# Latent attention: another order of TensorE's blocks in a step, and VectorE's front pieces moved

## The chip, the cores and the metric

The kernel runs on one core of one Trainium2 chip. The metric is the device time of one execution in microseconds; lower is better. TensorE (PE) multiplies matrices, its weight loads are shown as PEld; VectorE (DVE), ScalarE (ACT) and GpSimd (POOL) work element by element; SyncE (SP) issues the transfers. The engines run their own instruction queues in order and wait for one another on semaphores.

## The reference, cut to what matters

Two transformer layers run over x (16 sequences of 128 rows, 256 columns). The change touches the attention of the second one, and a part of the feed-forward's front that runs beside it.

```python
# x: (16, 128, 256), kv_c: (16, 128, 64); H = 16 heads, K = 128, D_C = 64, D_CQ = 192, R = 64
q_hk  = (layernorm(x) @ Wq.T)                      # per head 128
q_big = rope(einsum('bshk,hkq->bshq', q_hk, w_kc_q))   # per head 192
q_r   = einsum('bshq,hqr->bhsr', q_big, W_qr)
k_r   = einsum('bld,hdr->bhlr', rope(kv_c), W_kr)
attn  = softmax(einsum('bhsr,bhlr->bhsl', q_r, k_r))
ctx_c = einsum('bhsl,bld->bhsd', attn, rope(kv_c))
x    += einsum('bhsd,hkd->bhsk', ctx_c, w_kc_kv) @ Wo.T
# then: layernorm(x), quantised in blocks of 32 values (the "front"), and a feed-forward
```

## The kernel before

`latent_attention` folds the weights of each head: `a` is Wq times w_kc_q, `b` is W_qr times W_kr (so that keys need no projection of their own), `wc` is w_kc_kv times Wo. A step n handles one pair of heads for one group of four sequences: 8 pairs by 4 groups make 32 steps, and the loop over n has three more for what is still under way.

In a step TensorE computes three tiles of queries (`tile`, six matmuls each over 512 columns, as products of high and low parts). VectorE multiplies them by the rotary tables (`rotate_both` for tiles 0 and 1, `rotate_last`), GpSimd adds the products up (`add`), and in the next step TensorE makes the narrow product with `b` (`narrow_product`, 64 rows of output per head). ScalarE copies it to `qs` (`keep_narrow`, line 1446). Then come the scores (`score`, 64 rows of contraction per head), VectorE's maxima (`maximum`), ScalarE's exponentials (`exponential`), VectorE's reciprocals (`invert`), GpSimd's normalisation; TensorE transposes the probabilities (`turn_p`), ScalarE copies them (`keep_p`), TensorE multiplies them by the context (`context`, 64 rows of output per head), ScalarE copies the result and VectorE subtracts the copy, which leaves the low part (`keep_context`, `split_context`), and TensorE applies `wc` (`project`), accumulating over the eight pairs in two banks.

The order of the work is written out by hand, one list for each engine. Before, TensorE's list is

```python
                tile(n, 0); tile(n, 1); spare(n, 0); tile(n, 2); narrow_product(n - 1); spare(n, 1)
                turn_p(n - 2, 0); project(n - 3, 0); turn_p(n - 2, 1); project(n - 3, 1); spare(n, 2)
                score(n - 1); context(n - 2); spare(n, 3)
```

(the lines are joined here). `spare` holds what only some steps have. In steps 0 to 6 it folds the next pair's weights at its four places, each copied by ScalarE and split by VectorE before the next may use the one bank `w_ps`: queries' weights in two halves (`queries_weights`), context weights (`context_weights`, 64 rows of output per head), narrow weights. In steps 7, 15 and 23 it transposes the next group's rows in two halves (`turn`, `keep_rows`, `split_rows`). In steps 17, 25 and 33 it transposes the front's rows.

The front of group j is made in pieces, at fixed steps k after 8(j+1): VectorE's addition of the output to x (`f.add`, 2), statistics (3), with GpSimd's `deviations` (3), ScalarE's `f.normalise` (5), VectorE's block scales (6), division (7), clip and product (8), TensorE's transposes (9). Before, VectorE's pieces stand at the end of a step. ScalarE also normalises the next group's rows for this attention, in steps 1, 9 and 17 (`normalise`, line 1419). The front of the last group falls into the stage after.

Of the kernel before, what the change touches and what calls it, by code (L numbers as in the profile page):

```python
# [1128 lines left out]
def latent_attention(nc, m, f, d):  # L1129
# [6 lines left out]
    with ExitStack() as scope:  # L1136
# [20 lines left out]
        q_ps, w_ps = m.bank(6), m.bank(7)  # L1157
        ctx_ps, rows_ps = q_ps, m.ps16[:, 1, :]


        tile_bank = lambda n, k: (changing[n % 2], m.bank(1), changing[(n + 1) % 2])[k]
        scores_bank = lambda n, head: (changing[(n + 1) % 2], m.bank(3))[head]
        turned_p_bank = lambda n, head: (changing[n % 2], m.bank(3))[head]
        rows = [slice(0, CE), slice(CE, 2 * CE)]
# [19 lines left out]
        @block.sync  # L1184
        def _(sp):
            load_narrow(sp, m, d, 0)
            for i in range(1, PAIRS):
                wait(sp, c_made, i - 1)
                load_wide(sp, m, d, i)
                wait(sp, b_made, i - 1)  # L1190
                load_narrow(sp, m, d, i)

        @block.tensor
        def _(pe):
# [42 lines left out]
            def spare(n, place):  # L1237

                i, j, fj = weights_in(n), rows_in(n), front_in(n, 9)
                if i is not None:  # L1240
                    if place == 0:
                        wait(pe, b_kept, i)
                        if i == 1:
                            pe.wait_ge(y_lo, 1)
                        queries_weights(i, 0, w_ps)
                    elif place == 1:
                        pe.wait_ge(a_lo, 2 * i + 1)
                        queries_weights(i, 1, w_ps)
                    elif place == 2:
                        pe.wait_ge(a_lo, 2 * i + 2)  # L1250
                        context_weights(i, w_ps)
                    else:
                        pe.wait_ge(c_lo, i + 1)
                        narrow_weights(i, w_ps)
                if j is not None and place < 2:
# [5 lines left out]
                    turn(j, place, w_ps)  # L1261
                if fj is not None and place == 0:
                    pe.wait_ge(y_lo, 2 * min(fj + 2, GROUPS - 1) + 2)
                    f.turn(pe, m, fj, rows_ps)

            def tile(n, k):

                if inside(n, STEPS):
# [4 lines left out]
                    if k == 0 and i == 0:  # L1273
                        pe.wait_ge(y_lo, 2 * j + 2)
                    if k == 2:
                        if n == 0:
                            pe.wait_ge(c_lo, 1)
                        wait(pe, exp_made[0], n - 1)
                    else:
                        wait(pe, tile_turned, t - 2 * k)  # L1280
                    for kin in range(HALVES):
# [6 lines left out]
            def narrow_product(n):  # L1288

                if inside(n, STEPS):  # L1290
# [3 lines left out]
                    pe.wait_ge(q_made, 2 * n + 2)  # L1294
                    wait(pe, cs_lo, n - 1)
                    for head in range(2):
                        pe.matmul(q_ps[rows[head], :], b[i][:, 0, head * CE:(head + 1) * CE], q[n % 2][:, head, :],
                                  start=True, stop=False)
                    pe.matmul(q_ps, b[i][:, 1, :], q[n % 2][:, 2, :], start=False, stop=True).then_inc(narrowed, 1)  # L1299

            def turn_p(n, head):

                if inside(n, STEPS):
                    pe.wait_ge(normed[head], n + 1)
                    if head == 0:
                        pe.wait_ge(tile_turned, min(TILES * (n + 2) + 1, TILES * STEPS))
                    for s in range(4):
# [22 lines left out]
            def score(n):  # L1330

                if inside(n, STEPS):
                    if n == 0:
                        pe.wait_ge(c_lo, 1)
                    pe.wait_ge(qs_made, n + 1)
                    pe.wait_ge(tile_turned, min(TILES * (n + 1) + 1, TILES * STEPS))
                    for s in range(4):
                        for head in range(2):
                            if s == 0:
                                wait(pe, p_kept[head], n)  # L1340
                            t = pe.matmul(scores_bank(n, head)[:, s * S:(s + 1) * S], qs[rows[head], s * S:(s + 1) * S],  # L1341
# [4 lines left out]
            def context(n):  # L1346

                if inside(n, STEPS):
                    wait(pe, cs_lo, n)
                    for s in range(4):  # L1350
                        for head in range(2):
# [12 lines left out]
            for n in RUN:  # L1364
                tile(n, 0)
                tile(n, 1)
                spare(n, 0)
                tile(n, 2)
                narrow_product(n - 1)
                spare(n, 1)  # L1370
                turn_p(n - 2, 0)
                project(n - 3, 0)
                turn_p(n - 2, 1)
                project(n - 3, 1)
                spare(n, 2)
                score(n - 1)
                context(n - 2)
                spare(n, 3)

        @block.scalar  # L1380
        def _(act):
# [17 lines left out]
            def spare(n, place):  # L1399
                i, j, fj = weights_in(n), rows_in(n), front_in(n, 9)  # L1400
                if i is not None:
                    if place < 2:
                        keep_queries_weights(i, place, w_ps)
                    elif place == 2:
# [3 lines left out]
                if j is not None and place < 2:  # L1408
                    keep_rows(j, place, w_ps)
                if fj is not None and place == 0:  # L1410
                    f.keep(act, fj, rows_ps)
# [49 lines left out]
            for n in RUN:  # L1461
                exponential(n - 2, 0)
                keep_context(n - 3)
                exponential(n - 2, 1)
                spare(n, 0)
                keep_narrow(n - 1)
                spare(n, 1)
                keep_p(n - 2, 0)
                keep_p(n - 2, 1)
# [8 lines left out]
        def _(dve):  # L1478
# [21 lines left out]
            def spare(n, place):  # L1500
                i, j = weights_in(n), rows_in(n)
                if i is not None:
                    if place < 2:
                        split_queries_weights(i, place, w_ps)
                    elif place == 2:
                        split_context_weights(i, w_ps)
                if j is not None and place < 2:
                    split_rows(j, place, w_ps)

# [59 lines left out]
            for n in RUN:  # L1569
                maximum(n - 2, 0)  # L1570
                maximum(n - 2, 1)
                rotate_both(n, 0)
                invert(n - 2, 0)
                split_context(n - 3)
                rotate_both(n, 1)
                invert(n - 2, 1)
                spare(n, 0)
                rotate_last(n)
                spare(n, 1)
                spare(n, 2)  # L1580
                if n == 0:
                    last_statistics()
                for k, part in ((2, f.add), (3, f.statistics), (6, f.scales), (7, f.divide), (8, f.clip), (8, f.multiply)):
                    if front_in(n, k) is not None:
                        part(dve, m, front_in(n, k))

        @block.gpsimd
        def _(pool):
# [24 lines left out]
            for n in RUN:  # L1613
# [3 lines left out]
                if n == 0:  # L1617
# [6 lines left out]
                    pool.wait_ge(var_made, 4)  # L1624
                if front_in(n, 3) is not None:
                    f.deviations(pool, m, front_in(n, 3))
                    pool.wait_ge(f.var_made, VAR_STEPS * (front_in(n, 3) + 1))

# [560 lines left out]
```

## Time and profile before

| | |
|---|---|
| median of 3 runs | 831.03 us (829.92 to 831.12) |
| profiled execution | 830.3 us, of which the span from first to last instruction is 828.5 us |
| mean granted TensorE clock | 0.979 |
| latent stage, first tile to the start of the next stage | 352.6 to 741.2 us |

Times in the trace count from the span's first instruction. A matmul's record in the trace shows its form as rows\*columns of the array that its weights take, then the moving data as partitions x columns. Records of matmuls overlap, since they are pipelined, so the distance of one start to the next tells what a matmul costs, not its duration. A matmul in plain fp32 has two records.

### The profile page before, as it was taken

Reading aid. Unit: us, or ns where it says so; the run is one execution under the profiler, and the core shown is the slowest. Engines: PE = TensorE matmul, PEld = TensorE weight load, DVE = VectorE, ACT = ScalarE, POOL = GpSimd, SP = SyncE. Lnnn points to the kernel's source line nnn. Section 1 sums busy time; section 2 is a strip of 40 time slices with the busy share of each in tenths; the row PEclk is TensorE's granted clock in tenths of the full one; section 3 lists DMA queues with packets and bytes.
Section 4 is the critical chain, followed back from the end, with each engine's and each line's share of the span. In section 5 each row is a group of like instructions: output and inputs, shape, how many; then the busy total and the mean of one; then the engine's idle time right before and its main releaser. Section 6 shows DMA issues by size and latency. Waiting matters only on the chain. (4 is left out here: it accounts for less than half of the span.)

```text
span 828.5 us, 14817 instructions
## 1 busy us (share of the span) xinstructions
PE 754.8 (91%) x4808; PEld 539.7 (65%) x4808; DVE 611.7 (74%) x1083; ACT 403.6 (49%) x1068; POOL 571.5 (69%) x590
## 2 busy tenths in 40 slices
PE   4999999869999999788999999999999999876786
PEld 2555555447878887666777777777777777652564
DVE  5898999867887878665656666776678675749994
ACT  1688888533223222216545454655455445454453
POOL 5667776336676757555656778788877887817996
PEclk9999999989999999989999999999999999998999
DMA  9200000040000010122110000000000000000001
GB/s 258 109 1 0 0 0 1 2 169 20 20 19 20 19 57 0 51 103 96 48 49 1 1 1 1 2 2 1 1 1 1 2 1 1 1 2 7 25 32 40
DMA packets 8763, 24.12 MB, mean 29 GB/s; under 512 B 1711, under 2 KB 5167, under 8 KB 8087
## 3 DMA queue, kind: packets, MB, share of 16 engines
q1 hardware_dynamic: 8154, 23.28, 8.5%
q8 instruction: 33, 0.54, 0.3%
q14 instruction: 27, 0.22, 0.1%
q10 hardware_dynamic: 549, 0.08, 0.1%
HBM read 21.26 MB, written 2.10 MB: 28 GB/s over the span
## 5 line engine op out<-in xcount | busy, mean ns | idle before, releaser
L1606 POOL TENSOR_TENSOR q<-turned 64x512 f32<-64x512 f32 x128 | 168.1, 1313 | 25.7 <-DVE turned L1532 9.5
L1283 PE MATMUL ps<-l_yt,a 128*128 128x512 f32 x576 | 145.6, 403 | 2.1 <-ACT p L1429 1.6
L1283 PEld LDWEIGHTS ps<-l_yt,a 128*128 128x128 f32 x576 | 106.2, 190 | 27.4 <-issue 4.7
L1593 POOL TENSOR_TENSOR p<-p,l_inverse 128x512 f32<-128x512 f32 x64 | 66.8, 1047 | 74.2 <-DVE l_inverse L1554 73.7
L1429 ACT ACTIVATE p<-ps,l_negmax 128x128 f32<-128x128 f32 x256 | 91.1, 382 | 43.2 <-DVE l_negmax L1523 43.2
L1532 DVE TENSOR_TENSOR turned<-ps,rope 128x1024 f32<-128x1024 f32 x64 | 78.1, 1220 | 44.5 <-PE ps L1283 41.9
L871 PE MATMUL ps<-yt_experts,wsplit 128*128 (+1 forms) x384 | 99.2, 409 | 5.7 <-DVE h L974 5.2
L467 DVE TENSOR_REDUCE negmax<-ps 128x4 f32<-128x512 f32 x128 | 84.3, 685 | 12.9 <-PE ps L290 12.3
L871 PEld LDWEIGHTS ps<-yt_experts,wsplit 128*128 128x128 f32 x384 | 72.4, 195 | 23.6 <-issue 5.4
L383 ACT ACTIVATE pt<-ps 128x512 f32<-128x512 f32 x128 | 71.0, 599 | 6.3 <-PE ps L312 4.0
L1523 DVE TENSOR_REDUCE l_negmax<-ps 128x4 f32<-128x512 f32 x64 | 41.2, 686 | 44.3 <-PE ps L1341 44.1
L1544 DVE TENSOR_TENSOR turned<-ps,rope 64x512 f32<-64x512 f32 (+1 forms) x96 | 65.5, 683 | 2.1 <-PE ps L1283 0.7
L1446 ACT ACTIVATE qs<-ps 128x512 f32<-128x512 f32 x32 | 19.1, 597 | 98.1 <-PE ps L1299 98.1
L1073 POOL TENSOR_TENSOR ht<-h,ht 128x512 fp32r<-128x512 f32 x32 | 44.7, 1398 | 27.5 <-ACT ht L937 27.1
L1323 PE MATMUL ps<-wc,cs 128*128 128x256 f32 x384 | 62.0, 298 | 1.4 <-DVE cs L1560 1.4
L290 PE MATMUL ps<-bd,qt 96*128 96x512 f32 x128 | 56.5, 483 | 4.2 <-DVE negmax L467 2.6
L937 ACT ACTIVATE ht<-h 128x512 fp32r<-128x512 f32 x32 | 20.2, 632 | 80.2 <-DVE h L974 77.9
L894 PE MATMUL ps<-wsplit,ht 128*128 128x256 f32 x384 | 52.9, 288 | 6.7 <-POOL ht L1073 5.4
L894 PEld LDWEIGHTS ps<-wsplit,ht 128*128 128x128 f32 x384 | 50.7, 195 | 11.6 <-POOL ht L1073 7.6
L1429 ACT ACTIVATION_READ_ACCUMULATOR p<-ps,l_negmax 128x1 f32 x256 | 56.9, 222 | 0.0
L1323 PEld LDWEIGHTS ps<-wc,cs 128*128 128x128 f32 x384 | 50.5, 192 | 1.7 <-DVE cs L1560 1.7
L312 PE MATMUL ps<-qt,bd 104*128 104x512 f32 x128 | 51.6, 429 | 0.0
(213 smaller groups left out, 1567.0 us busy)
## 6 DMA issues: line engine op xcount, KB each, us to landing
wide<-in_wide SPq DMA_DIRECT2D x8, 768.0 KB, 4.5
mx_raw<-in_mx SPq DMA_DIRECT2D x8, 384.0 KB, 3.1
x<-in_x SPq DMA_DIRECT2D x4, 512.0 KB, 8.9
ctx_t<-in_ctx_t SPq DMA_DIRECT2D x1, 2048.0 KB, 7.6
out<-x SPq DMA_DIRECT2D x16, 128.0 KB, 1.7
narrow<-in_narrow SPq DMA_DIRECT2D x8, 192.0 KB, 2.6
ktraw<-in_ctx_rows SPq DMA_DIRECT2D x1, 1248.0 KB
wraw<-in_gate SPq DMA_DIRECT2D x1, 1024.0 KB, 18.4
```

The source lines that it names most:

```text
L290: pe.matmul(scores[k % 2], qt[par][0:QROWS, half, g, :], bd[par][0:QROWS, half, :, :].rearrange("p k t -> p (k t)"), start=True, stop=True ...
L383: act.activation(pt[i][:, :], scores_t[i % 3], ACT.Exp, scale=scale).then_inc(exp_made, 1)
L467: dve.tensor_reduce(negmax[par][:, g, half * KV4:(half + 1) * KV4], scores[k % 2].rearrange("s (k t) -> s k t", k=KV4), AX.X, ALU.max, neg ...
L871: t = pe.matmul(out, w_at(pw, w + k * EXPERTS * INTER + x * INTER, INTER), run_of(m.yt[:, py, k, :, :], j).rearrange("p b s -> p (b s)"), ...
L894: t = pe.matmul(down_ps[:, s, :], ht[par][:, ph, s * S:(s + 1) * S], w_at(pw, 4 * FFN + expert * E, E), start=(expert == 0 and q == 0 and ...
L1283: out = pe.matmul(tile_bank(n, k), a[i][:, pa, kin, k * 128:(k + 1) * 128], yt[j % 2][:, py, kin, :, :].rearrange("p b s -> p (b s)"), sta ...
L1323: t = pe.matmul(proj_ps[:, half, s * E:(s + 1) * E], cs[n % 2][:, pc, (2 * half + s) * S:(2 * half + s + 1) * S], wc[:, pw, i, :], start=( ...
L1429: t = act.activation(p[:, head, s, :], scores_bank(n, head)[:, s * S:(s + 1) * S], ACT.Exp, bias=negmax[:, head, s:s + 1], accum_out=total ...
L1532: dve.tensor_tensor(turned[:, 2 * k:2 * k + 2, :].rearrange("p t (b s) -> p t b s", b=4), spread(tile_bank(n, k).rearrange("p (b s) -> p b ...
L1544: r = dve.tensor_tensor(turned[out_rows, k, :].rearrange("p (b s) -> p b s", b=4), tile_bank(n, 2)[in_rows, :].rearrange("p (b s) -> p b s ...
L1593: pool.tensor_tensor(p[:, head, :, :], p[:, head, :, :], spread(inverse[:, head, :], 2, S), ALU.mult).then_inc(normed[head], 1)
L1606: t = pool.tensor_tensor(out[rows[(head + half) % 2], head, :], turned[rows[head], half, :], turned[rows[head], 2 + half, :], ALU.add)
```

## The change

TensorE's list becomes: tiles 0 and 1, spare 0, tile 2, narrow product of step n-1, spare 1, context of n-3, scores of n-1, both transposes of probabilities of n-2, spare 2, both outputs of n-3, spare 3. Context thus comes one step later than before, in the same step as its output. The third narrow product is issued head by head. Banks are exchanged: context goes to tile 1's bank, the second head's transposed probabilities to the narrow product's. In `spare` the context weights move to place 1, the second half of the queries' weights to place 2, the second half of a group's rows and the front's transposes to place 2. VectorE makes the front's pieces between the maxima and the first rotation, at k = 3, 4, 6, 7, 8 and 9. The waits follow the banks, and SP waits for one more event before it loads a pair's weights.

```diff
-        ctx_ps, rows_ps = q_ps, m.ps16[:, 1, :]
+        ctx_ps, rows_ps = m.bank(1), m.ps16[:, 1, :]
-        turned_p_bank = lambda n, head: (changing[n % 2], m.bank(3))[head]
+        turned_p_bank = lambda n, head: (changing[(n + 1) % 2], q_ps)[head]
...
                 wait(sp, c_made, i - 1)
+                wait(sp, a_made, 2 * (i - 1))
                 load_wide(sp, m, d, i)
...
-                    if k == 2:
+                    if k == 0:
+                        wait(pe, tile_turned, TILES * n)
+                        wait(pe, p_kept[0], n - 2)
+                    elif k == 1:
+                        wait(pe, tile_turned, TILES * (n - 1) + 2)
+                        wait(pe, cs_lo, n - 3)
+                    else:
                         if n == 0:
                             pe.wait_ge(c_lo, 1)
                         wait(pe, exp_made[0], n - 1)
-                    else:
-                        wait(pe, tile_turned, t - 2 * k)
...
-                    wait(pe, cs_lo, n - 1)
+                    wait(pe, p_kept[1], n - 1)
...
-                    pe.matmul(q_ps, b[i][:, 1, :], q[n % 2][:, 2, :], start=False, stop=True).then_inc(narrowed, 1)
+                    for head in range(2):
+                        t = pe.matmul(q_ps[rows[head], :], b[i][:, 1, head * CE:(head + 1) * CE], q[n % 2][:, 2, :],
+                                      start=False, stop=True)
+                    t.then_inc(narrowed, 1)
...
                     if head == 0:
-                        pe.wait_ge(tile_turned, min(TILES * (n + 2) + 1, TILES * STEPS))
+                        pe.wait_ge(tile_turned, min(TILES * (n + 3), TILES * STEPS))
+                    else:
+                        pe.wait_ge(qs_made, min(n + 2, STEPS))
...
+                    wait(pe, p_kept[0], n - 1)
+                    wait(pe, exp_made[1], n)
                     for s in range(4):
                         for head in range(2):
-                            if s == 0:
-                                wait(pe, p_kept[head], n)
...
                     wait(pe, cs_lo, n)
+                    pe.wait_ge(tile_turned, min(TILES * (n + 3) + 2, TILES * STEPS))
...
                 spare(n, 1)
+                context(n - 3)
+                score(n - 1)
                 turn_p(n - 2, 0)
+                turn_p(n - 2, 1)
+                spare(n, 2)
                 project(n - 3, 0)
-                turn_p(n - 2, 1)
                 project(n - 3, 1)
-                spare(n, 2)
-                score(n - 1)
-                context(n - 2)
                 spare(n, 3)
...
                 exponential(n - 2, 0)
-                keep_context(n - 3)
                 exponential(n - 2, 1)
                 spare(n, 0)
                 keep_narrow(n - 1)
                 spare(n, 1)
+                keep_context(n - 3)
...
                 maximum(n - 2, 0)
                 maximum(n - 2, 1)
+                for k, part in ((3, f.add), (4, f.statistics), (6, f.scales), (7, f.divide), (8, f.clip), (9, f.multiply)):
+                    if front_in(n, k) is not None:
+                        part(dve, m, front_in(n, k))
                 rotate_both(n, 0)
                 invert(n - 2, 0)
-                split_context(n - 3)
                 rotate_both(n, 1)
                 invert(n - 2, 1)
                 spare(n, 0)
                 rotate_last(n)
                 spare(n, 1)
+                split_context(n - 3)
                 spare(n, 2)
                 if n == 0:
                     last_statistics()
-                for k, part in ((2, f.add), (3, f.statistics), (6, f.scales), (7, f.divide), (8, f.clip), (8, f.multiply)):
-                    if front_in(n, k) is not None:
-                        part(dve, m, front_in(n, k))
...
-                if front_in(n, 3) is not None:
-                    f.deviations(pool, m, front_in(n, 3))
-                    pool.wait_ge(f.var_made, VAR_STEPS * (front_in(n, 3) + 1))
+                if front_in(n, 4) is not None:
+                    f.deviations(pool, m, front_in(n, 4))
+                    pool.wait_ge(f.var_made, VAR_STEPS * (front_in(n, 4) + 1))
```

## Rows read from the trace of the kernel before

**Rows 1.** The page's first part: busy time, share of the span, instructions.

```profile
PE 754.8 (91%) x4808; PEld 539.7 (65%) x4808; DVE 611.7 (74%) x1083; ACT 403.6 (49%) x1068; POOL 571.5 (69%) x590
```

**Rows 2.** Stretches, steps 3, 12: length, busy PE, PEld, DVE, ACT, POOL; granted clock, DMA.

```profile
391.26:404.86 13.60, 13.60 (x104) 10.45 (x102) 7.88 (x13) 6.72 (x24) 9.32 (x8) 1.00 0.21 75
500.78:511.63 10.85, 10.85 (x78) 8.05 (x76) 6.34 (x11) 5.06 (x21) 10.04 (x12) 1.00 0.01 2
```

**Rows 3.** Timeline of TensorE, step 12: start, time, line, form, count.

```profile
500.78 4.40 PE L1283 MATMUL ps<-l_yt,a 128*128 128x512 f32 x18
505.11 1.08 PE L1297 MATMUL ps<-q,b 128*64 128x512 f32 x4
506.12 1.12 PE L1299 MATMUL ps<-q,b 128*128 128x512 f32 x2
507.08 0.60 PE L1308 MATMUL ps<-ident,p 128*128 128x128 f32 x4
...
508.24 0.60 PE L1308 MATMUL ps<-ident,p 128*128 128x128 f32 x4
...
509.48 1.20 PE L1341 MATMUL ps<-keys,qs 64*128 64x128 f32 x16
510.61 1.09 PE L1354 MATMUL ps<-l_pt,kvr 128*64 128x128 f32 x16
511.63 0.50 PE L1283 MATMUL ps<-l_yt,a 128*128 128x512 f32 x1
```

**Rows 4.** The same timeline cut inside blocks: first record still running, how many remain.

```profile
501.81 3.37 PE L1283 MATMUL ps<-l_yt,a 128*128 128x512 f32 x14
...
503.64 1.54 PE L1283 MATMUL ps<-l_yt,a 128*128 128x512 f32 x6
...
506.65 0.59 PE L1299 MATMUL ps<-q,b 128*128 128x512 f32 x1
...
507.88 0.52 PE L1323 MATMUL ps<-wc,cs 128*128 128x256 f32 x3
...
509.74 0.94 PE L1341 MATMUL ps<-keys,qs 64*128 64x128 f32 x13
...
510.07 0.61 PE L1341 MATMUL ps<-keys,qs 64*128 64x128 f32 x7
```

**Rows 5.** Timeline of the other engines in step 12.

```profile
503.69 0.66 DVE L1560 TENSOR_TENSOR cs<-ps,cs 128x512 fp32r<-128x512 f32 x1
...
505.48 2.06 DVE L1544 TENSOR_TENSOR turned<-ps,rope 128x512 f32<-128x512 f32 x3
...
506.92 5.27 POOL L1606 TENSOR_TENSOR q<-turned 64x512 f32<-64x512 f32 x4 [0.23 <-POOL p L1593]
...
507.28 0.60 ACT L1446 ACTIVATE qs<-ps 128x512 f32<-128x512 f32 x1 [3.35 <-PE ps L1299]
...
510.67 1.29 DVE L1523 TENSOR_REDUCE l_negmax<-ps 128x4 f32<-128x512 f32 x2 [3.12 <-PE ps L1341]
```

**Rows 6.** The page's groups: the exponentials, busy us, mean ns, idle before.

```profile
L1429 ACT ACTIVATE p<-ps,l_negmax 128x128 f32<-128x128 f32 x256 | 91.1, 382 | 43.2 <-DVE l_negmax L1523 43.2
```

**Rows 7.** Timeline: the front's normalisation and scales, first group.

```profile
520.22 2.06 ACT L1700 ACTIVATE f_y<-x,f_shift,f_rstd 128x256 f32<-128x256 f32 x4
...
529.29 1.22 DVE L1712 TENSOR_REDUCE f_yscale<-f_y 128x32 f32<-128x1024 f32 x1
...
531.31 1.29 DVE L1633 TENSOR_SCALAR f_yscale<-f_yscale 128x32 f32<-128x32 f32 x1
```

**Rows 8.** Timeline of the stage's end: last tiles, last scores, front's product, last output.

```profile
709.84 0.50 PE L1283 MATMUL ps<-l_yt,a 128*128 128x512 f32 x1
...
725.03 1.94 DVE L1731 TENSOR_TENSOR f_yq<-f_yc,f_yscale 128x1024 bf16<-128x1024 bf16 x1
...
727.87 1.20 PE L1341 MATMUL ps<-keys,qs 64*128 64x128 f32 x16
...
739.18 1.70 PE L1323 MATMUL ps<-wc,cs 128*128 128x256 f32 x12 [1.42 <-DVE cs L1560]
```

More of the change, by code:

```diff
@@ L1247, in spare @@
                         pe.wait_ge(a_lo, 2 * i + 1)
+                        context_weights(i, w_ps)
+                    elif place == 2:
+                        pe.wait_ge(c_lo, i + 1)
                         queries_weights(i, 1, w_ps)
-                    elif place == 2:
+                    else:
                         pe.wait_ge(a_lo, 2 * i + 2)
-                        context_weights(i, w_ps)
-                    else:
-                        pe.wait_ge(c_lo, i + 1)
                         narrow_weights(i, w_ps)
-                if j is not None and place < 2:
+                if j is not None and place in (0, 2):
                     if place == 0:
@@ L1260, in spare @@
                         pe.wait_ge(y_lo, 2 * j + 1)
-                    turn(j, place, w_ps)
-                if fj is not None and place == 0:
+                    turn(j, place // 2, w_ps)
+                if fj is not None and place == 2:
                     pe.wait_ge(y_lo, 2 * min(fj + 2, GROUPS - 1) + 2)
@@ L1278, in tile @@
                         wait(pe, exp_made[0], n - 1)
-                    else:
-                        wait(pe, tile_turned, t - 2 * k)
                     for kin in range(HALVES):
@@ L1305, in turn_p @@
                     if head == 0:
-                        pe.wait_ge(tile_turned, min(TILES * (n + 2) + 1, TILES * STEPS))
+                        pe.wait_ge(tile_turned, min(TILES * (n + 3), TILES * STEPS))
+                    else:
+                        pe.wait_ge(qs_made, min(n + 2, STEPS))
                     for s in range(4):
@@ L1401, in spare @@
                 if i is not None:
-                    if place < 2:
-                        keep_queries_weights(i, place, w_ps)
-                    elif place == 2:
+                    if place in (0, 2):
+                        keep_queries_weights(i, place // 2, w_ps)
+                    elif place == 1:
                         keep_context_weights(i, w_ps)
@@ L1407, in spare @@
                         keep_narrow_weights(i, w_ps)
-                if j is not None and place < 2:
-                    keep_rows(j, place, w_ps)
-                if fj is not None and place == 0:
+                if j is not None and place in (0, 2):
+                    keep_rows(j, place // 2, w_ps)
+                if fj is not None and place == 2:
                     f.keep(act, fj, rows_ps)
@@ L1502, in spare @@
                 if i is not None:
-                    if place < 2:
-                        split_queries_weights(i, place, w_ps)
-                    elif place == 2:
+                    if place in (0, 2):
+                        split_queries_weights(i, place // 2, w_ps)
+                    else:
                         split_context_weights(i, w_ps)
-                if j is not None and place < 2:
-                    split_rows(j, place, w_ps)
+                if j is not None and place in (0, 2):
+                    split_rows(j, place // 2, w_ps)
             def last_statistics():
```

## The prediction

> **What bounds the kernel now.** I began with the page: TensorE is busy most of the span [rows 1]. An average says nothing of one stage, so I cut the latent stage into steps by the starts of tile 0. Steps 3 to 6, which also make the next pair's weights, last 13.60 us; steps from 7 on last 10.85 us; in both kinds TensorE is busy for the whole step at a granted clock of 1.00, its 2.4 GHz level, and GpSimd, the next fullest engine, for 10.04 of 10.85 us at its worst [rows 2]. So in these steps nobody keeps TensorE waiting. Its time is what its own instructions take, and moving a wait can gain nothing there. What could gain is TensorE's own pace.
>
> The timeline of one step gives each block's slot, from its start to the next one's [rows 3]: tiles 4.33, first two narrow products 1.01, third 0.96, transposes and output twice, 1.16 and 1.24, scores 1.13, context 1.02; together 10.85. Cuts inside the blocks give the pace without the edges [rows 4]: tiles (503.64 - 501.81)/8 = 0.229 each, so 18 take 4.12; a pass of the narrow product at 512 columns 507.08 - 506.65 = 0.43, so two passes for the pair and two for the third make 1.72; a scores record (510.07 - 509.74)/6 = 0.055, so 16 take 0.88, and I give context's 16 records, of the same 128 columns, the same. Transposes and output without an edge are 1.16 twice, 2.32. Sum 9.92. The other 0.93 us of the step lies at edges, and the forms in the rows say which: tiles 128\*128 to narrow 128\*64, 128\*64 to 128\*128 inside the narrow product, output 128\*128 to scores 64\*128, scores to context 128\*64, context to tiles. Transposes and output, both 128\*128, alternate without one: an output matmul takes (508.24 - 507.88)/3 = 0.12, six take 0.72, and of 1.16 that leaves 0.11 for each of four transposes, what two scores records of 128 columns take [rows 3, 4]. So a change of the array's shape costs 0.93/5 = 0.186 us. By block the losses are tiles 0.21, narrow 0.25, output to scores 0.08, scores 0.25, context 0.14.
>
> **The change, part by part.**
>
> *TensorE's order.* Each step runs tiles (128\*128), narrow and context (128\*64, the third product now split by head into that form too), scores (64\*128), then transposes, output and the next tiles (all 128\*128). That is three changes of shape for five: -2 x 0.186 = -0.37 us, so 10.48 us. Scores to transposes, narrow to context and output to tiles stand in no row here. I price the first as any other change and the other two at nothing, as between transposes and output. From a change at half price to one at the dearest block's 0.25, the saving lies between 0.2 and 0.5. Steps 3 to 6 had one more, since the context weights are 128\*64 by the source: six for three, -0.56. Steps 7 to 30: 24 x -0.37 = -8.9. Steps 3 to 6: 4 x -0.56 = -2.2.
>
> *The split product.* It issues one more matmul. If its two heads share the array as the first two products do (four records of 128\*64 in 1.01 us, as long as two of 128\*128 in 0.96 [rows 3]), the same two passes of 0.43 remain. The Trainium skill (TensorE: Matmul & The Clock Gate, "The mechanism") says that a weight load overlaps a running matmul only where the row groups differ, and these two heads use the same rows; by that rule the halves would follow one another, which the pair in the trace does not do.
>
> *New waits.* Offsets in the new step from tile 0's start, by the paces above: narrow 4.22, its last pass 5.56, context 5.99, scores 6.97, transposes 8.1, output 9.1, end 10.48.
> - Scores need the copy of the narrow product with only context between. The copy starts 0.63 after the last pass starts (507.28 - 506.65) and takes 0.60 [rows 4, 5], so it is done at 6.79: 0.18 early. This is the thinnest cover.
> - Output needs the same step's context, copied and split: context's results 7.1, copy 0.60, split 0.66 [rows 5], 8.4 against 9.1.
> - Transposed probabilities go where tile 2 was: VectorE's last rotation began 4.70 after tile 0 and took 2.06 [rows 3, 5], so 6.8 against 8.1. Context needs tile 1's rotation, done near 4.3.
> - Behind the scores: VectorE's maxima follow the split, 8.4 + 1.29 = 9.7 [rows 5]; ScalarE's eight exponentials start at 9.9, after the two copies of turned probabilities, and at 0.36 each [rows 6] end at 12.8, or 2.3 into the next step. Reciprocals still follow the rotations; GpSimd's additions, 5.27 and one more of a quarter of that [rows 5], end near 12.3, and narrow wants them at 14.7.
> - SP's extra wait holds back the wide and narrow loads behind it by one place, some 4 us, with over a step until their first reader: nothing.
>
> *Places where a cover is gone.*
> - Steps 7, 15, 23 turn the next group's second half after the transposed probabilities. Turned, copied (0.60, behind two other copies) and split, it is done near 11.55, and tile 0 could start at 11.37: 3 x 0.2 = +0.6.
> - ScalarE's two normalisations (2.06 [rows 7]) come just before the exponentials, which free tile 2's bank. In steps 10, 14, 22, 30 the first four end at 9.9 + 2.06 + 1.5 - 10.48 = 3.0 against tile 2 at 2.85: 4 x 0.1 = +0.4. In step 18 the wide copy of the front's rows precedes them too (twice 0.60 less the slack): +0.6.
> - VectorE's pieces stand before the first rotation. From 9.7 to the rotation at 1.7 of the next step there is 2.4 us, and the addition, statistics, division, clip and product (the longest about 1.94 [rows 8]) fit. The scales in steps 14, 22 and 30 do not: they need ScalarE's normalised rows, at 1.5. Their reduction takes 1.22 [rows 7], three small instructions some 0.8, so rotations start at 3.55, 1.9 late; context then waits 0.3 for tile 1's rotation and the transposes 0.15 for the last: 3 x 0.45 = +1.4. In the trace one of the small ones takes 1.29 [rows 7], while GpSimd adds; here GpSimd has run dry, waiting for the reciprocal behind them. At full length for all, each such step would lose about 2.1. The Trainium skill (SBUF — State Buffer, "Who interferes with whom") has VectorE's tensor_scalar and GpSimd exclude each other for a whole instruction; that agrees with the 1.29, and by it a GpSimd addition still running would bring the larger price.
>
> *Start.* Steps 0 to 2 have nothing to put between the second half of the queries' weights and the narrow weights, whose copy and split take about 1.2; against that step 2 loses context to step 3. I take +0.4, between -0.5 and +1.5.
>
> *End.* Before, from tile 0 of the last step to the last output is 739.18 - 709.84 = 29.34, of which 18.03 to the last scores [rows 8]. After, GpSimd finishes the last sums at about 12.4, narrow, context and scores follow without transposes and output between: 15.1. From there the chain is maxima, VectorE's product of the front's (1.94 [rows 8]) ahead of the reciprocals, normalisation, transposes, output of step 30, context and output: 12.25 against 11.31. Together -2.0.
>
> **Sum.** -8.9 - 2.2 + 0.6 + 0.4 + 0.6 + 1.4 + 0.4 - 2.0 = -9.7 us. The profiled execution took 830.3 us, so 820.6; the median of the runs stands 0.7 above it, so 821 us.
>
> **Rivals.**
> - *The edges do not go away* (the loss belongs to a block's beginning whatever stood before, or scores to transposes costs as much as two). For it: scores lose 0.25 and narrow 0.25, more than the mean. Against it: transposes and output follow one another without loss [rows 3, 4]. Then the steps stay at 10.85, and the lost covers (+3.4) meet the end's -2.0: 832 us, no change.
> - *The halves of the split product follow one another.* The third product would take four passes, 1.72 for 0.86: 32 x 0.86 = 27.5 us more, 849 us, slower. It decides once the halves overlap less than two thirds, since 0.3 us a step is what the forecast has to lose. Against it: the first two products' records.
> - *Scores wait for the narrow copy.* The cover is 0.18 us; each 0.1 us beyond it costs 3.2 us over 32 steps. With 0.15 us late, 826 us: still faster. For it: a release costs a few hundredths that I have not counted.
> - *VectorE's pieces cost their full length* in steps 14, 22, 30 : +5 us, 826 us.
>
> **How the numbers follow.** My forecast (816 to 826 us) has 0.62, more gain than that 0.05, late scores 0.10, long pieces 0.06, edges that stay 0.10, halves in a row with anything else that costs 0.3 us a step 0.07. The likeliest gives 821. Two tenths are left out with 813 to 829: the low end is 0.5 us a step, the high end 0.2 us a step with the longer stalls. A change of 0.2% (1.7 us) is about what can be told from none. Faster takes the first four, 0.83; the edges' tenth is shared, 0.06 same and 0.04 slower; with the last, slower is 0.11.
>
> **What would show it.** After: steps of about 10.5 us with TensorE still busy throughout, steps 3 to 6 of about 13.05; four records each of two forms become eight of 128\*64 in the narrow product, in about 1.8 us; context directly behind it without an edge; tile 0 directly behind output. Wrong would be: steps of 10.85; a wait of TensorE for the copy of line 1446 in every step; a narrow product of 2.7 us; or waits for tile 1's rotation in more than three steps.

## The result, and the profile after

The changed kernel takes 823.81 us (median of 5 runs, 822.83 to 825.62) against 831.03: ratio 0.9914, 95% interval 0.9888 to 0.9939. The forecast was 821.0, range 813 to 829. The profiled execution took 825.62 us, with a span of 823.8 us. In this section and below, a step's length is the distance of two starts of tile 0, and "the end" runs from tile 0 of the last step to the first matmul of the next stage.

The page's first part, the line that answers to [rows 1]:

```profile
PE 749.3 (91%) x4872; PEld 539.8 (66%) x4872; DVE 609.9 (74%) x1083; ACT 405.2 (49%) x1068; POOL 571.4 (69%) x590
```

64 more TensorE records are the split product, 32 matmuls of two records each. TensorE is busy 5.5 us less. The stretches of steps 5 and 12, as in [rows 2]:

```profile
406.69:419.79 13.10, 13.10 (x105) 10.49 (x104) 8.12 (x15) 6.73 (x24) 8.44 (x7) 1.00 0.23 79
499.62:510.05 10.43, 10.43 (x81) 7.97 (x80) 7.46 (x17) 5.10 (x23) 8.50 (x8) 1.00 0.00 0
```

The steps fell from 13.60 to 13.10 and from 10.85 to 10.43 (most of the plain ones measure 10.42), and TensorE is still busy for the whole of both. TensorE's timeline of step 12, against [rows 3]:

```profile
499.62 4.30 PE L1288 MATMUL ps<-l_yt,a 128*128 128x512 f32 x18
...
503.85 1.08 PE L1302 MATMUL ps<-q,b 128*64 128x512 f32 x4
...
504.76 1.03 PE L1305 MATMUL ps<-q,b 128*64 128x512 f32 x4
...
505.62 1.04 PE L1365 MATMUL ps<-l_pt,kvr 128*64 128x128 f32 x16
...
506.59 1.16 PE L1351 MATMUL ps<-keys,qs 64*128 64x128 f32 x16
...
507.69 1.09 PE L1318 MATMUL ps<-ident,p 128*128 128x128 f32 x8
...
508.53 1.68 PE L1333 MATMUL ps<-wc,cs 128*128 128x256 f32 x12
...
510.05 0.40 PE L1288 MATMUL ps<-l_yt,a 128*128 128x512 f32 x1
```

Slots, start to start: tiles 4.23, narrow 1.77, context 0.97, scores 1.10, transposes and outputs 2.36. Against the forecast's pace without edges the losses are 0.11, 0.05, 0.09, 0.22 and 0.04, together 0.51 for three changes of shape: 0.17 each on average, where five cost 0.93 before. The slots do not share it evenly. The scores in front of the transposes lose 0.22; the tiles in front of the narrow product lose 0.11 where the same pair of blocks lost 0.21 before. So the price of a change is an average, and none is shown for a single edge. Eight narrow records take 1.77 us: the split product's halves shared the array. The other engines in that step, against [rows 5]:

```profile
505.84 0.60 ACT L1457 ACTIVATE qs<-ps 128x512 f32<-128x512 f32 x1 [3.99 <-PE ps L1305]
506.59 0.97 PEld L1351 LDWEIGHTS ps<-keys,qs 64*128 64x128 f32 x16 [0.17 <-ACT qs L1457]
...
509.35 0.37 ACT L1440 ACTIVATE p<-ps,l_negmax 128x128 f32<-128x128 f32 x1
```

The copy ends at 506.44 and the scores' weights load at 506.59, 0.15 us later; the scores start 6.97 us into the step, as forecast. How much of the 0.15 is cover shows in the run with a slower copy, below. The exponentials begin 9.73 into it (forecast 9.9).

The end, against [rows 8]:

```profile
702.62 4.36 PE L1288 MATMUL ps<-l_yt,a 128*128 128x512 f32 x18
...
716.51 1.37 PE L1302 MATMUL ps<-q,b 128*64 128x512 f32 x4 [3.18 <-POOL q L1622]
717.66 1.93 PE L1305 MATMUL ps<-q,b 128*64 128x512 f32 x4
719.37 1.64 PE L1365 MATMUL ps<-l_pt,kvr 128*64 128x128 f32 x16
720.94 1.16 PE L1351 MATMUL ps<-keys,qs 64*128 64x128 f32 x16
...
733.03 1.70 PE L1333 MATMUL ps<-wc,cs 128*128 128x256 f32 x12 [1.42 <-DVE cs L1571]
```

The last narrow product starts 13.89 us after tile 0 (forecast 12.4), the last scores at 18.32 (15.1), the last output at 30.41 against 29.34 before. TensorE waits 3.18 us for GpSimd's sums, and narrow and context then take 4.43 us where step 12 has 2.74. That stretch, as in [rows 2]:

```profile
716.51:720.94 4.43, 4.43 (x24) 2.23 (x25) 0.00 (x0) 0.60 (x1) 1.95 (x2) 0.61 0.00 0
```

The granted clock (third from the end) was 0.61 in it, behind the idle time: a mix of the 1.2 and the 2.4 GHz level. Why the sums are late, from the timelines of VectorE and GpSimd:

```profile
693.43 1.22 DVE L1723 TENSOR_REDUCE f_yscale<-f_y 128x32 f32<-128x1024 f32 x1 [2.24 <-ACT f_y L1711]
...
695.51 1.22 DVE L1543 TENSOR_TENSOR turned<-ps,rope 128x1024 f32<-128x1024 f32 x1
...
701.83 1.23 DVE L1729 TENSOR_TENSOR f_y<-f_y,f_yinverse 128x1024 fp8e4<-128x1024 f32 x1
705.65 1.23 DVE L1543 TENSOR_TENSOR turned<-ps,rope 128x1024 f32<-128x1024 f32 x1 [2.60 <-PE ps L1288]
...
712.28 1.72 DVE L1736 TENSOR_SCALAR f_yc<-f_y 128x1024 bf16<-128x1024 fp8e4 x1
```

```profile
505.24 5.28 POOL L1617 TENSOR_TENSOR q<-turned 64x512 f32<-64x512 f32 x4 [0.23 <-POOL p L1604]
...
699.36 6.19 POOL L1617 TENSOR_TENSOR q<-turned 64x512 f32<-64x512 f32 x4 [0.23 <-POOL p L1604]
...
709.51 5.61 POOL L1617 TENSOR_TENSOR q<-turned 64x512 f32<-64x512 f32 x4 [0.23 <-POOL p L1604]
```

The first rotation of the last step starts 3.03 after tile 0; step 12 has it at 1.59. The view names tile 0 as what it waited for, but that was long done. GpSimd's additions of the step before end at 699.36 + 6.19 = 705.55, right ahead of it: `rotate_both` waits on `q_made`, since `turned` is one buffer. Those additions are late from their start. In step 30 (tile 0 at 692.01) the front's scales hold the first rotation back until 695.51, 3.50 us into the step; the four additions begin 7.35 us into it, where step 12 has 5.62 and 5.28 us for them, and beside the division they take 6.19.

### The profile page after: what moved, and what is told of

The parts are those of the page before. It is cut to its first block and busy times, and to the rows that moved or that the text cites. A ratio compares the mean times of both kernels' runs of the same rounds, so it can differ in the third digit from the quotient of the medians.

```text
span 823.8 us, 15063 instructions
## 1 busy us (share of the span) xinstructions
PE 749.3 (91%) x4872; PEld 539.8 (66%) x4872; DVE 609.9 (74%) x1083; ACT 405.2 (49%) x1068; POOL 571.4 (69%) x590
## 5 line engine op out<-in xcount | busy, mean ns | idle before, releaser
L467 DVE TENSOR_REDUCE negmax<-ps 128x4 f32<-128x512 f32 x128 | 84.3, 685 | 12.4 <-PE ps L290 11.7
L894 PEld LDWEIGHTS ps<-wsplit,ht 128*128 128x128 f32 x384 | 50.7, 195 | 11.7 <-POOL ht L1073 7.7
L1333 PE MATMUL ps<-wc,cs 128*128 128x256 f32 x384 | 53.6, 288 | 1.4 <-DVE cs L1571 1.4
L1464 ACT ACTIVATE l_pt<-ps 128x512 f32<-128x512 f32 x64 | 35.0, 597 | 34.6 <-PE ps L1318 34.6
L1571 DVE TENSOR_TENSOR cs<-ps,cs 128x512 fp32r<-128x512 f32 x32 | 22.2, 692 | 37.2 <-ACT cs L1449 37.1
```

Source lines behind the costliest of these rows:

```text
L467: dve.tensor_reduce(negmax[par][:, g, half * KV4:(half + 1) * KV4], scores[k % 2].rearrange("s (k t) -> s k t", k=KV4), AX.X, ALU.max, neg ...
L894: t = pe.matmul(down_ps[:, s, :], ht[par][:, ph, s * S:(s + 1) * S], w_at(pw, 4 * FFN + expert * E, E), start=(expert == 0 and q == 0 and ...
L1333: t = pe.matmul(proj_ps[:, half, s * E:(s + 1) * E], cs[n % 2][:, pc, (2 * half + s) * S:(2 * half + s + 1) * S], wc[:, pw, i, :], start=( ...
```

## The experiments

Intervals are of the ratio to the kernel before.

**Before, with the third narrow product split.** The rest is the kernel before.

```diff
-                    pe.matmul(q_ps, b[i][:, 1, :], q[n % 2][:, 2, :], start=False, stop=True).then_inc(narrowed, 1)
+                    for head in range(2):
+                        t = pe.matmul(q_ps[rows[head], :], b[i][:, 1, head * CE:(head + 1) * CE], q[n % 2][:, 2, :],
+                                      start=False, stop=True)
+                    t.then_inc(narrowed, 1)
```

> The kernel before with one part of the change alone: the third narrow product is issued head by head. By my theory what counts is how often the array's shape changes in a step. Here it stays five times: the change from 128*64 to 128*128 only moves from inside the narrow product to its end, before the transposes. So steps 8 to 14 stay at 10.85 us (within 0.06) and the time within 0.3% of before. By the rival, that the wide third product itself is slow (it loses 0.2 us in the slot that it shares), the split alone takes about 0.2 us from each of 32 steps: steps of 10.65 us and 6.4 us less.

830.93 us, ratio 0.9981 (0.9949 to 1.0013). TensorE, step 12:

```profile
504.57 1.08 PE L1297 MATMUL ps<-q,b 128*64 128x512 f32 x4
505.48 1.03 PE L1300 MATMUL ps<-q,b 128*64 128x512 f32 x4
506.44 0.66 PE L1311 MATMUL ps<-ident,p 128*128 128x128 f32 x4
```

The edge only moves: narrow now takes 1.87 for 1.97, but the transposes behind it are of another shape. Five changes stay, and the step stays (10.82 for 10.85). A form that saved time by itself would have shown it here.

**After, without the split** (the edit above, undone).

> The changed kernel with the third narrow product whole again, in one matmul of 128*128. By the count of shapes, a step now changes shape five times instead of three (into 128*128 and back to 128*64 for context): steps of 10.42 + 2 x 0.2 = 10.8 us, and of the 7.2 us that the change gained nearly all is gone (28 steps x 0.4 = 11 us, more than the gain, so 1 to 5 us above before). By the rival, that only the product itself is slower, steps of 10.6 us and 6 us more than the changed kernel, still about 1 us under before.

833.77 us, ratio 1.0033 (1.0002 to 1.0063); steps 3 to 6 take 13.45.

```profile
503.22 1.08 PE L1302 MATMUL ps<-q,b 128*64 128x512 f32 x4
504.23 1.12 PE L1304 MATMUL ps<-q,b 128*128 128x512 f32 x2
505.29 1.09 PE L1362 MATMUL ps<-l_pt,kvr 128*64 128x128 f32 x16
```

The order alone, with five changes of shape, gains nothing (plain steps 10.78 to 10.84): the third product stands as an island between two 128\*64 blocks and costs 2.07 with the pair, where 1.77 was, and context's slot grows from 0.97 to 1.02. Order and split are worth something only together.

**After, with transposes and outputs alternating** as before.

```diff
                 turn_p(n - 2, 0)
+                project(n - 3, 0)
                 turn_p(n - 2, 1)
                 spare(n, 2)
-                project(n - 3, 0)
                 project(n - 3, 1)
```

> The changed kernel with transposes and output interleaved by head, as before the change. The shapes are the same three, so by the count of shapes nothing moves: steps of 10.42 us (within 0.06), and the time of the changed kernel, 0.991 of before. By the rival, that every block's beginning costs, two more beginnings cost 0.2 to 0.4 us a step: 10.6 to 10.8 us, 6 to 12 us more.

834.25 us, ratio 1.0026 (0.9999 to 1.0052). The plain steps are 10.42, as the count of shapes has it, but the total was missed: steps 3 to 6 take 13.79, steps 7, 15, 23 12.2 to 12.3, steps 10, 14, 18, 22, 30 from 11.3 to 11.7, the end 35.5. Two more beginnings of blocks, of the shape before them, cost a plain step nothing, so it is not a block's beginning that costs. ScalarE in step 12, then TensorE in step 10:

```profile
513.48 0.60 ACT L1464 ACTIVATE l_pt<-ps 128x512 f32<-128x512 f32 x1 [1.07 <-PE ps L1318]
514.64 0.60 ACT L1464 ACTIVATE l_pt<-ps 128x512 f32<-128x512 f32 x1 [0.56 <-PE ps L1318]
515.14 0.36 ACT L1440 ACTIVATE p<-ps,l_negmax 128x128 f32<-128x128 f32 x1
```

```profile
486.45 1.67 PE L1288 MATMUL ps<-l_yt,a 128*128 128x512 f32 x6 [0.53 <-ACT p L1440]
```

The second copy comes after an output, so the exponentials begin 10.40 us into the step (tile 0 at 504.74) for 9.73. Where ScalarE has more to do, tile 2 waits for its bank. Both transposes in one go is what keeps the exponentials on time.

**After, with the copy of the narrow product in eight pieces.**

```diff
-                    act.activation(qs[:, :], q_ps, ACT.Copy).then_inc(qs_made, 1)
+                    for c in range(8):
+                        t = act.activation(qs[:, c * 64:(c + 1) * 64], q_ps[:, c * 64:(c + 1) * 64], ACT.Copy)
+                    t.then_inc(qs_made, 1)
```

> The changed kernel, in which ScalarE copies the narrow product in eight pieces of 64 columns instead of one of 512, so that the copy that the scores wait for ends about 0.4 us later (a copy of 512 columns takes 0.60 us, one of 256 takes 0.38, which leaves about 0.16 for each instruction). If the cover in front of the scores is the 0.18 us that I worked out, TensorE waits about 0.2 to 0.3 us in each of 32 steps: steps of 10.6 to 10.7 us, 6 to 10 us more than the changed kernel. If the cover is larger than I think (by the rival that GpSimd and VectorE pace the step by now), nothing moves: 10.42 us.

833.66 us, ratio 1.0027 (0.9996 to 1.0058). ScalarE's copy and the scores in step 12, and the waits of TensorE over steps 8 to 29:

```profile
508.73 1.04 ACT L1458 ACTIVATE qs<-ps 128x64 f32<-128x64 f32 x8 [4.05 <-PE ps L1305]
```

```profile
509.82 1.16 PE L1351 MATMUL ps<-keys,qs 64*128 64x128 f32 x16 [0.27 <-ACT qs L1458]
```

```profile
PE ps L1351 <- ACT qs L1458: 5.9, 22, 0.3
```

The copy takes 0.44 longer. Plain steps take 10.77 to 10.83, and steps 7 to 30 are 8.4 us longer in all, 0.35 each: about 0.1 of the 0.44 was covered, not 0.18. The lines agree. Here the copy ends at 509.77 and the scores, which wait for it, start at 509.82, so the release takes 0.05 us; of the 0.15 us between the two in the changed kernel 0.10 are cover. That the changed kernel's scores do not wait for the copy shows in the run without the split as well: there the copy ends 0.32 us ahead of the scores, and in both kernels they follow context's last record by 0.20 us.

**After, with the front's scales at the end of step 6** instead of the start.

```diff
-                for k, part in ((3, f.add), (4, f.statistics), (6, f.scales), (7, f.divide), (8, f.clip), (9, f.multiply)):
+                for k, part in ((3, f.add), (4, f.statistics), (7, f.divide), (8, f.clip), (9, f.multiply)):
...
                 spare(n, 2)
+                if front_in(n, 6) is not None:
+                    f.scales(dve, m, front_in(n, 6))
```

> The changed kernel with VectorE's block scales back at the end of step 6, where ScalarE's normalised rows have long been made, so that the rotations of steps 14, 22 and 30 start on time. My theory of the end: GpSimd's additions of the last step come late because VectorE rotates into one buffer, each rotation waits for the additions before it, and the scales' 1.9 us in step 30 with the division's contention in step 31 use up the slack of that loop. Then the end is about 1.5 us shorter, 30.9 instead of 32.4, its first narrow product at about 12.6 after tile 0 instead of 13.9; steps 14, 22 and 30 keep 10.6, since ScalarE's exponentials hold them, and the whole is 1 to 2 us faster than the changed kernel. By the rival, that the end only waits for GpSimd's own work, it stays at 32.4.

824.04 us, ratio 0.9902 (0.9864 to 0.994); the changed kernel, measured beside it, 824.37, 0.9919 (0.9887 to 0.9951). The steps stay (15 and 23 are 0.2 longer), and so does the end (32.8, the last narrow product at 14.25), which had been expected shorter. VectorE ahead of the last step, whose tile 0 starts at 701.41:

```profile
699.31 1.21 DVE L1725 TENSOR_REDUCE f_yscale<-f_y 128x32 f32<-128x1024 f32 x1
700.55 1.28 DVE L1645 TENSOR_SCALAR f_yscale<-f_yscale 128x32 uint32<-128x32 uint32 x1
...
702.47 1.29 DVE L1534 TENSOR_REDUCE l_negmax<-ps 128x4 f32<-128x512 f32 x2
703.68 1.22 DVE L1731 TENSOR_TENSOR f_y<-f_y,f_yinverse 128x1024 fp8e4<-128x1024 f32 x1
704.81 1.22 DVE L1543 TENSOR_TENSOR turned<-ps,rope 128x1024 f32<-128x1024 f32 x1
```

The place was badly chosen: a small instruction takes 1.28 us beside GpSimd's additions (0.18 in step 30 of the changed kernel, where none runs beside it), maxima and division follow late, and the rotation comes 3.40 after tile 0. The lateness moved from GpSimd's queue to VectorE's, so this run didn't separate theory and rival.

**The one before, with ScalarE's normalisations behind the exponentials** of the next step.

```diff
                 spare(n, 0)
+                if n % PAIRS == 2 and n // PAIRS < GROUPS - 1:
+                    normalise(n // PAIRS + 1)
+                if front_in(n, 6) is not None:
+                    f.normalise(act, m, front_in(n, 6))
...
-                if n % PAIRS == 1 and n // PAIRS < GROUPS - 1:
-                    normalise(n // PAIRS + 1)
-                if front_in(n, 5) is not None:
-                    f.normalise(act, m, front_in(n, 5))
```

> The kernel with the scales at the step's end, and in addition ScalarE's two normalisations moved from the end of their step to the gap behind the exponentials of the next one, where ScalarE waits some 4 us for the narrow product. My theory: the normalisations delay the exponentials, and these tile 2, in steps 10, 14, 18, 22 and 30. Then these steps take 10.42 (step 18 too, 11.0 before), 1.3 us less in all, and nothing else moves: 2 to 3.5 us faster than the changed kernel, about 820.5 us. By the rival, that VectorE or GpSimd holds these steps, they stay.

820.64 us, ratio 0.9863 (0.9825 to 0.9902); measured again, 819.56, 0.9861 (0.9814 to 0.9908). Steps 10, 14, 22 and 30 fall from 10.61, step 18 from 11.00, all to at most 10.48, so it was the exponentials' delay that made them long. Not foreseen: step 2 falls from 14.40 to 12.53, since the table load ahead of the exponentials no longer stands behind a normalisation there: it begins at 379.94 us here, at 381.84 in the changed kernel, whose tile 2 then waits 1.67 us for the exponentials; here it doesn't wait.

**After, with VectorE's pieces but the addition back at a step's end** (k = 3, 6, 7, 8, 8).

```diff
-                for k, part in ((3, f.add), (4, f.statistics), (6, f.scales), (7, f.divide), (8, f.clip), (9, f.multiply)):
+                for k, part in ((3, f.add),):
...
+                for k, part in ((3, f.statistics), (6, f.scales), (7, f.divide), (8, f.clip), (8, f.multiply)):
+                    if front_in(n, k) is not None:
+                        part(dve, m, front_in(n, k))
```

> The changed kernel with this part undone: VectorE's pieces of the front (all but the addition) stand at the end of a step again, in front of the maxima, at the old step numbers. By my theory the place of the pieces is not where the gain comes from: steps without pieces stay at 10.42, those after a piece of 2 to 3 us get exponentials 2 to 3 us later, which tile 2 notices by 0 to 0.7 us in steps 12, 15, 16, 17 and their like, so 0 to 5 us more than the changed kernel, less the 1.5 us at the end that the scales cost there. By the rival, that the change owes its gain to VectorE's order, all of the 7 us are gone.

831.63 us, ratio 1.0003 (0.9978 to 1.0029), 7.3 us above the changed kernel beside it, where 0 to 5 had been expected. Plain steps stay at 10.42, as the theory has it; steps 16, 17, 24, 25 rise to 12.1 to 12.3 (from 10.5 to 11.0), and the end, expected shorter, to 35.9. The latent stage is 9.6 us longer. VectorE, then TensorE, step 16:

```profile
542.00 2.29 DVE L1732 TENSOR_TENSOR f_y<-f_y,f_yinverse 128x1024 fp8e4<-128x1024 f32 x1
544.22 1.27 DVE L1534 TENSOR_REDUCE l_negmax<-ps 128x4 f32<-128x512 f32 x2
```

```profile
546.48 1.66 PE L1288 MATMUL ps<-l_yt,a 128*128 128x512 f32 x6 [1.29 <-ACT p L1440]
```

In the new order maxima are due at a step's end. A piece ahead of them (the division, 2.29 us) delays the exponentials, and tile 2 waits 1.29 us. So the shorter plain steps do not come from the pieces' new place, but without it what they gain is lost elsewhere. The new place in the kernel before was not run, and what lengthens the end here was not followed.

**The front's last group out of the end's way**, on top of the moved normalisations.

```diff
-                    if front_in(n, k) is not None:
+                    if front_in(n, k) is not None and (k in (3, 4, 9) or n < STEPS - 1):
...
                 spare(n, 1)
+                if n == STEPS:
+                    dve.wait_ge(q_made, 2 * STEPS)
+                    f.scales(dve, m, GROUPS - 2)
+                    f.divide(dve, m, GROUPS - 2)
                 split_context(n - 3)
                 spare(n, 2)
-                if front_in(n, 6) is not None:
+                if n == STEPS:
+                    f.clip(dve, m, GROUPS - 2)
+                elif front_in(n, 6) is not None and n < STEPS - 2:
                     f.scales(dve, m, front_in(n, 6))
```

> On top of the kernel with the moved normalisations, the scales, the division and the clip of the last group that lies inside the stage leave steps 30 to 32: VectorE makes scales and division in step 32 only once GpSimd has made the last sums, the clip behind the split of the context of step 29. Groups 0 and 1 stay as they were; the arithmetic is the same. My theory: the first rotation of a step waits for GpSimd's additions of the step before, since VectorE has one buffer for turned rows, so what slows GpSimd in steps 30 and 31 pushes the last narrow product. Then the first rotation of step 31 starts at about 1.7 us after tile 0 (3.0 in the changed kernel), the last narrow product at about 12.5 us (13.9), the last output at about 30.9 us (32.6 in the kernel with the moved normalisations), the stage is about 1.7 us shorter, and the kernel takes about 819 us. Rival: GpSimd's own work, additions of 5.3 us and the fifth one, holds the end whatever VectorE does: the last narrow product stays at 13.9 and the end at 32 to 33 us. A second rival: the late pieces only move the wait to the front's turn behind them, and the end is longer than 32.6.

816.93 us, ratio 0.9832 (0.9797 to 0.9868), against 0.9861 for the kernel without this edit, measured beside it. VectorE, GpSimd and TensorE in the end (tile 0 of the last step at 696.90):

```profile
698.50 1.23 DVE L1543 TENSOR_TENSOR turned<-ps,rope 128x1024 f32<-128x1024 f32 x1 [2.42 <-PE ps L1288]
...
713.65 0.69 DVE L1744 TENSOR_SCALAR f_yc<-f_y 128x1024 bf16<-128x1024 fp8e4 x1
```

```profile
702.56 5.27 POOL L1625 TENSOR_TENSOR q<-turned 64x512 f32<-64x512 f32 x4 [0.23 <-POOL p L1612]
```

```profile
709.23 1.08 PE L1302 MATMUL ps<-q,b 128*64 128x512 f32 x4 [1.69 <-POOL q L1630]
710.14 1.03 PE L1305 MATMUL ps<-q,b 128*64 128x512 f32 x4
710.99 1.04 PE L1365 MATMUL ps<-l_pt,kvr 128*64 128x128 f32 x16
711.97 1.16 PE L1351 MATMUL ps<-keys,qs 64*128 64x128 f32 x16
...
724.30 1.70 PE L1333 MATMUL ps<-wc,cs 128*128 128x256 f32 x12 [1.42 <-DVE cs L1571]
```

The stretch of the last narrow product and context, as in [rows 2]:

```profile
709.23:711.97 2.74, 2.74 (x25) 1.43 (x25) 2.15 (x6) 0.96 (x4) 1.94 (x2) 1.00 0.00 0
```

The rotation comes 1.60 after tile 0, the last narrow product 12.33, the last scores 15.07, the last output 27.40; the end is 29.6 for 32.4 in the changed kernel and 32.6 and 32.9 in the two executions with the moved normalisations. The rival, GpSimd's own work, would have left it at 32 to 33, the second rival above 32.6. The last output comes earlier than the expected 30.9. Of the 3.01 us that it gains on the changed kernel, 1.56 are the earlier sums and 1.69 the clock: narrow and context take 2.74 us at a granted clock of 1.00 here, 4.43 at 0.61 in the changed kernel (4.43 x 0.61 = 2.70); the chain behind them is 0.24 longer. TensorE's wait ahead of them is 1.69 us here and 3.18 there, but the length of the wait does not settle the clock: with the slow copy it is 2.69 us and the clock 1.00, with the pieces at a step's end 2.48 and 0.66. That the clock holds because the pieces moved is not shown.

## Why the prediction was right, and where it was not

The mechanism was right: fewer changes of shape shorten every step, at about the price that was worked out. The total came out at 823.8 for 821 partly by luck: the end went the other way by 3.1 us, and the edges and the front's delays, 1.4 and 1.0 better than forecast, made up for most of it. The terms, forecast and measured between the profiled executions (us):

| term | forecast | measured |
|---|---|---|
| steps 7 to 30, edges | -8.9 | 24 x -0.43 = -10.3 |
| steps 3 to 6 | -2.2 | -2.0 |
| steps 7, 15, 23 | +0.6 | +0.9 (11.6 for 11.73) |
| step 18 | +0.6 | +0.6 |
| steps 10, 14, 22, 30 | +0.4 and +1.4 | 4 x 0.19 = +0.8 |
| steps 8, 16, 24 and others | 0 | +0.5 |
| start | +0.4 | +0.75 |
| end | -2.0 | +1.07 |
| latent stage | -9.7 | -7.7 |

(the others' 0.5 is what remains of the 24 steps' -7.56.)

- **The edges** carried the forecast and were as it said: plain steps with five changes of shape are 10.78 to 10.85 in three kernels of two orders, with three they are 10.41 to 10.49 in all the others but the one with the slow copy. Narrow to context and output to tiles cost next to nothing (0.05 and 0.04). Scores to transposes, priced as any other, is the dearest at 0.22, twice the other two, as one rival feared; the sum still held. That the edges would stay is refuted.
- **The halves** of the split product ran together, 1.77 us for eight records. (Before there were four records of 128\*64 and two of 128\*128 [rows 3], not four of each, as the prediction's signs have it.) The rule of the Trainium skill (TensorE: Matmul & The Clock Gate, "The mechanism") that a weight load overlaps only with a matmul of other rows does not hold for them: their weights load at 504.33, together with the start of records of the first two products that use the same 128 rows, and the next records start at 504.76. With the halves in a row, as the prediction read that rule, the product would take 0.86 more in each step.
- **Late scores**: 0.10 of the 0.18 of cover were left; most of the difference is the release that the forecast had not counted, 0.05 us. The plain steps show no wait for it.
- **The scales** were sized wrongly. Their instructions took what was said (the rotation of step 14 came 3.59 into the step, forecast 3.55), yet context didn't wait, and the 0.19 is the exponentials', as moving the normalisations shows. Tile 1's rotation follows the first at once and ends 6.01 us into the step, where context was due at 5.99, so the 0.3 priced for it is not there.
- **The end** is the term that failed: "GpSimd finishes the last sums at about 12.4". That is a plain step's time (12.26 in step 12). The forecast had the scales delay the rotations of step 30 but did not carry it into step 31, whose rotations wait for GpSimd's additions of step 30. The additions of steps 30 and 31 were slowed besides, to 6.19 and 5.61 us, with VectorE's division and clip beside them. The trace of before already shows a last narrow product at 13.66, which the forecast did not use. The last output came 3.06 us later than forecast (30.41 for 27.35): 1.49 are the sums (13.89 for 12.4), 1.73 the narrow product and context, which took 4.43 us at a clock of 0.61 where the forecast had 2.7, and the chain behind was 0.16 shorter. The forecast reckoned with the full clock, which the kernel before has in that place (1.00, behind a wait of 2.74 us); why it fell in one and not in the other stays open. With the pieces out of the way the forecast's own numbers come out, 15.07 for 15.1 and 27.40 for 27.35; the run removes lateness of VectorE's queue as well, so it does not divide it between the two engines.
- **The start**: the forecast's 0.4 belonged to steps 0 to 2, for the second half of the queries' weights, but step 2 stayed at 14.40. The 0.75 comes from step 0, which took 10.67 to 11.95 us in the executions of kernels that share this part, so it says nothing for the term.
- **Outside the stage**: the span fell by only 4.6 us, since the stages ahead took 1.6 and the feed-forward stage 1.5 longer in this execution, both in code that the change doesn't touch. The second profiled execution of the changed kernel has the long feed-forward stage too, but not the later start. The medians differ by 7.2.

## What to carry to other kernels

Where one engine is busy for a whole step, cut its timeline into slots and compare them with its pace inside the blocks: here 0.93 of 10.85 us was lost where the array's shape changed, and putting blocks of one shape side by side won 0.43 of it back. Reordering the bound engine moves the due times of everyone else: the shorter steps did not need the pieces' new place, but without that move their whole gain was lost. At the end of a pipeline, read when the last inputs are really made, and by whom; moving a side job that is nearly free in the loop went with 3 us there, about half of them the clock's.

## What the runs showed of the hardware

- A change of the array's shape costs TensorE 0.17 to 0.21 us on average (0.51 for three, 0.93 for five; 0.42 for two, without the split), with no wait shown for it. Single slots lose 0.08 to 0.25.
- VectorE and GpSimd slow one another in both directions: VectorE's clip takes 1.72 us beside GpSimd's additions and 0.69 without. The division takes 2.29 us in one kernel; in another it takes 1.23, and GpSimd's four additions go from 5.27 to 6.19. The Trainium skill (SBUF — State Buffer, "Who interferes with whom") says that a VectorE instruction with two inputs in SBUF contends with GpSimd's reads, as the division shows.
- The feed-forward stage, the same code in all kernels, took 85.4 to 88.8 us, close to 85.5, 87.2 or 88.8 in each profiled execution. The three of 88.8 have a granted clock of 0.90 in the stage, the others 0.94 to 0.96; what picks the length was not tried.
